# Decoder layer: k and v of cross-attention computed inside self-attention, and a cross-attention loop with the context product two pairs behind the scores

## The reference, cut to what matters

```
# self-attention: 16 heads of 32
scores = (q k^T + q . pos_emb[l-r] + k . pos_emb[l-r]) / sqrt(32)
ctx    = softmax(scores) v ;  h = ctx @ Wo + bo + x ; layer norms -> x1
# cross-attention: 16 heads of 64, batch 8 x 512 seen as (8, 512)
q = x1 Wq[h] + bq[h] ; k = context Wk[h] + bk[h] ; v = context Wv[h] + bv[h]
out = softmax(causal(q k^T / sqrt(64))) v ;  out @ Wo + bo ; add, norm
```

## Time and profile before

| | |
|---|---|
| median of 3 runs | 4272.65 us (4272.12 to 4275.99) |
| the profiled execution | 4274.03 us, span 4272.1 us, granted clock 0.942 |
| PE busy | 3681.4 us (86%) |
| DVE, ACT, POOL busy | 2230.7 (52%), 1678.6 (39%), 1859.8 us (44%) |
| self-attention, 0 to 1700 us | PE busy 1435 us, DMA share 0.96 |
| cross-attention, 1905 to 3107 us | PE busy 1154 us, DMA share 0.53 |

### The profile page before, as it was taken

The page is one execution under the profiler, slowest core; times in us unless marked ns, Lnnn a source line. Parts: engine busy times, 40 slices in busy tenths (PEclk is TensorE's granted clock), DMA queues, the critical chain, the costliest instruction groups (busy, mean ns, idle before and its releaser), DMA issues. The chain is left out here.

```text
span 4272.1 us, 67667 instructions
## 1 busy us (share of the span) xinstructions
PE 3681.4 (86%) x19584; PEld 2298.4 (54%) x19584; DVE 2230.7 (52%) x6128; ACT 1678.6 (39%) x3639; POOL 1859.8 (44%) x1684
## 2 busy tenths in 40 slices
PE   6988888888888886769999999999989987788686
PEld 4766666667676674325556666655545552122244
DVE  4666676767666665773554555455523231111155
ACT  4666666666666664333333333333312110000023
POOL 3766666667676665433444444444511100000012
PEclk9999999999999998989999999999989998898798
DMA  6999999999999997455555555555355328999723
GB/s 246 399 375 391 386 385 374 386 369 386 373 388 377 385 387 295 142 176 194 180 180 175 173 172 176 179 178 180 128 183 186 107 74 350 420 421 421 290 79 118
DMA packets 544321, 1151.74 MB, mean 270 GB/s; under 512 B 34240, under 2 KB 206912, under 8 KB 494912
## 3 DMA queue, kind: packets, MB, share of 16 engines
q1 hardware_dynamic: 539520, 1141.13, 71.7%
q10 hardware_dynamic: 4032, 7.34, 0.5%
q0 software_dynamic: 512, 0.26, 0.0%
HBM read 745.46 MB, written 403.18 MB: 269 GB/s over the span
## 5 line engine op out<-in xcount | busy, mean ns | idle before, releaser
L433 POOL TENSOR_SCALAR a_sc<-a_sc,a_inv 128x512 f32<-128x512 f32 x512 | 818.5, 1602 | 383.1 <-DVE a_inv L383 313.1
L1004 POOL TENSOR_SCALAR b_sc<-b_sc,b_inv 128x128 f32<-128x128 f32 (+3 forms) x512 | 549.6, 1082 | 657.5 <-DVE b_inv L957 657.5
L284 ACT ACTIVATE a_stage_q<-a_ps_q 128x640 f32<-128x640 f32 x512 | 360.0, 703 | 469.8 <-PE a_ps_q L201 442.5
L962 DVE COPY b_pt<-b_ps_t 128x128 f32<-128x128 f32 (+3 forms) x512 | 250.2, 489 | 547.3 <-PE b_ps_t L863 547.3
L390 DVE COPY a_pt<-a_ps_t 128x512 f32<-128x512 f32 x512 | 353.6, 691 | 280.3 <-PE a_ps_t L187 242.3
L376 DVE CUSTOM_DVE_ANT_0 a_sc<-a_ps_s,a_rq 128x512 f32<-128x512 f32 x512 | 353.9, 691 | 197.2 <-PE a_ps_s L177 145.0
L918 ACT ACTIVATE b_sc<-b_sc,b_mx 128x128 f32<-128x128 f32 (+3 forms) x512 | 281.0, 550 | 446.7 <-DVE b_mx L951 446.7
L274 ACT ACTIVATE a_sc<-a_sc,a_mx 128x512 f32<-128x512 f32 x512 | 370.5, 724 | 77.5 <-DVE a_mx L376 75.9
L175 PE MATMUL a_ps_s<-a_ks,a_qs 128*128 128x512 f32 x512 | 261.2, 510 | 139.4 <-DMA a_rk<-band_k 103.9
L284 ACT ACTIVATE a_stage_k<-a_ps_k 128x640 f32<-128x640 f32 x512 | 359.1, 701 | 30.4 <-DMA band_k<-a_stage_k 30.4
L187 PEld LDWEIGHTS a_ps_t<-a_ident,a_sc 128*128 128x128 f32 x2048 | 249.9, 145 | 218.2 <-issue 201.2
(11 more groups left out here) (200 smaller groups left out, 6159.5 us busy)
## 6 DMA issues: line engine op xcount, KB each, us to landing
band_q<-a_stage_q SPq DMA_DIRECT2D x128, 1280.0 KB, 9.0
band_k<-a_stage_k SPq DMA_DIRECT2D x128, 1280.0 KB, 11.6
a_rk<-band_k SPq DMA_DIRECT2D x128, 1024.0 KB, 13.9
a_rq<-band_q SPq DMA_DIRECT2D x256, 512.0 KB, 14.6
d_w<-in_e_W SPq DMA_DIRECT2D x32, 4096.0 KB, 36.9
b_xT<-x1T SPq DMA_DIRECT2D x64, 1024.0 KB, 5.7
b_cT<-in_ctxT SPq DMA_DIRECT2D x64, 1024.0 KB, 8.4
d_wg<-in_e_Wg SPq DMA_DIRECT2D x16, 4096.0 KB, 28.0
```

Of the source, the lines that this page charges most:

```text
L284: act.activation(st[h % 2][:, t, :].rearrange("p (a n) -> p a n", a=2), src[:, :, 0:WIN // 2], ACT.Copy).then_inc(sem[f"a_{kind}_staged"], 1)
L433: pool.tensor_scalar(sc[n][:, :], sc[n][:, :], inv[:, n:n + 1], None, ALU.mult)\
L1004: pool.tensor_scalar(sc[i][:, 0:width(i)], sc[i][:, 0:width(i)], inv[:, i:i + 1], None, ALU.mult).then_inc(sem["b_normed"], 1)
```

## The change

Four things are changed together.

1. The k and v of cross-attention are projected in self-attention. Each quad takes two pairs: 16 parts m (four for k of the first pair, four for its v, and the same for the second), put at the ticks in `KV_AT`. Each result is copied by ScalarE to one tile kv, which SyncE stores to DRAM scratch. ScalarE issues the loads of the weights (okv, 512 KB each) and, once in four quads, of the context (oc, 1 MB).
2. To find PSUM for it, ps_q and ps_k share three banks, and the bands are four products of 384, 256, 256 and 384 columns. To find SBUF, pt holds two heads instead of four, so that the context product of self-attention is made in two halves (ticks 11 and 3), each with the sums of r = 0, 1 and r = 2, 3 in rows of their own, which VectorE then adds.
3. cross_attention projects only q. k and v are loaded from the scratch, the bias of v is added by ScalarE when it copies the context product out.
4. The loop of cross_attention is staggered otherwise: in pair n TensorE does the scores of n, the transposes of n-1, the context product of n-2 at i = 0, and the projection of q for n+1 at i = 1, 2, 5 and 7. sc, mx, sm and inv are doubled, pt is single.

```diff
-Q_AT, K_AT, HI_AT = [5, 6, 7, 8], [10, 11, 12, 13], [9, 14]
+Q_AT, K_AT, HI_AT = {5: [0], 6: [1], 7: [2], 8: [3]}, {13: [0, 1], 14: [2, 3]}, [9, 15]
+CX_AT, CX_OUT_AT = [HALF + LAG_A, LAG_A], [HALF + LAG_A + 1, LAG_A + 1]
+KV_AT = [[1, 2, 3, 4, 5, 6, 7, 8, 9, 10, 11, 11, 12, 13, 14, 15], list(range(NT)), list(range(NT)),
+         [0, 1, 2, 3, 4, 4, 5, 6, 7, 7, 8, 9, 10, 10, 11, 12]]
...
+            def store_kv(g, n):
+                sp.wait_ge(sem["a_kv_out"], 4 * g + n + 1)
+                settle()
+                sp.dma_start(dr[("b_k", "b_v")[n % 2]](2 * g + n // 2), kv[:, :]).then_inc(sem["a_kv_stored"], 16)
             def quad(g, j):
                 for h in range(HQ):
+                    if inside(g):
+                        store_kv(g, h)
                     if inside(g + 1):
                         write(g + 1, (j + 1) % 4, h)
...
+            def project_kv(g, j, m):
+                c, kind, n = m // 8, m // 4 % 2, m % 4
+                if m == 0 and j == 0:
+                    pe.wait_ge(sem["a_oc_in"], 4 * g + 16)
+                if m % 8 == 0:
+                    pe.wait_ge(sem[f"a_okv_in{c}"], 16 * g + 16)
+                if n == 0 and counts(4 * g + m // 4):
+                    pe.wait_ge(sem["a_kv_out"], 4 * g + m // 4)
+                if kind == 0:
+                    mm = pe.matmul(ps_o[:, :], okv[c][:, 0, n, :], oc[:, n, :], start=(n == 0), stop=(n == K4 - 1))
+                else:
+                    for k in range(K4):
+                        mm = pe.matmul(ps_o[:, n * P:(n + 1) * P], oc[:, k, n * P:(n + 1) * P], okv[c][:, 1, k, :],
+                                       start=(k == 0), stop=(k == K4 - 1))
...
+            def kv_out(g, j, n):
+                act.wait_ge(sem["a_kv_ready"], 4 * g + n + 1)
+                if counts(4 * g + n):
+                    act.wait_ge(sem["a_kv_stored"], 16 * (4 * g + n))
...
+                if n == 3 and j == 3 and inside(g + 1):
+                    act.dma_start(oc[:, :, :], dr["a_oc"](g + 1)).then_inc(sem["a_oc_in"], 16)
+                if n % 2 and inside(g + 1):
+                    act.dma_start(okv[n // 2][:, :, :, :].rearrange("p a k n -> p (a k n)"),
+                                  dr["b_wkv"](2 * ((j + 1) % 4) + n // 2)).then_inc(sem[f"a_okv_in{n // 2}"], 16)
...
 cross_attention, SyncE
+            def load(n, j):
+                if not early(n, 2):
+                    sp.wait_ge(sem["b_q_ready"], n - 1)
+                    settle()
+                    sp.wait_ge(sem["b_score"], NP * (n - 1))
+                    settle()
+                s = sem[f"b_in{j % 2}"]
+                sp.dma_start(wq[j % 2][:, :, :].rearrange("p k n -> p (k n)"), dr["b_wq"](n)).then_inc(s, 16)
+                sp.dma_start(xT[j % 2][:, :, :], dr["x1T"](n)).then_inc(s, 16)
+                if not early(n, 4):
+                    sp.wait_ge(sem["b_cx_out"], n - 3)
+                    settle()
+                sp.dma_start(cols[j][:, :], dr["b_cols"](n)).then_inc(s, 16)
+                sp.dma_start(kT[j % 2][:, :], dr["b_k"](n)).then_inc(s, 16)
+            def load_v(n, j):
+                if not early(n, 2):
+                    sp.wait_ge(sem["b_cx_ready"], n - 1)
+                    settle()
+                sp.dma_start(v[j % 2][:, :, :].rearrange("p t n -> p (t n)"), dr["b_v"](n))\
+                    .then_inc(sem[f"b_v_in{j % 2}"], 16)
+            def store(n, j):
+                sp.wait_ge(sem["b_cx_out"], n + 1)
...
+            def pair(n, j):
+                if inside(n + 1) and not early(n, 1):
+                    load(n + 1, (j + 1) % 4)
+                if not early(n, 2):
+                    store(n - 2, (j - 2) % 4)
+                if inside(n + 1) and not early(n, 1):
+                    load_v(n + 1, (j + 1) % 4)
...
 cross_attention, TensorE
+            def project_q(n, j, k):
+                if k == 0:
+                    pe.wait_ge(sem[f"b_in{j % 2}"], (n - j % 2) * 32 + 64)
+                    if not early(n, 1):
+                        pe.wait_ge(sem["b_q_out"], n)
...
+            def pair(n, j):
+                for i in range(NP):
+                    if i in (0, 4) and inside(n):
+                        scores(n, j, i)
+                    if i == 0 and not early(n, 2):
+                        context(n - 2, j % 2)
+                    if not early(n, 1):
+                        turn(n - 1, (j - 1) % 4, i)
+                    if i in Q_OF_PAIR and inside(n + 1):
+                        project_q(n + 1, (j + 1) % 4, Q_OF_PAIR.index(i))
...
 cross_attention, ScalarE and VectorE
+            def pair(n, j):
+                for i in range(NP):
+                    if inside(n):
+                        softexp(n, j, i)
+                    if i == 3 and not early(n, 2):
+                        cx_out(n - 2, (j - 2) % 4)
+                if inside(n + 1):
+                    q_out(n + 1, (j + 1) % 4)
...
+            def pair(n, j):
+                for half in (0, 4):
+                    if inside(n):
+                        for i in range(half, half + 4):
+                            add_max(n, j, i)
+                    for i in range(half, half + 4):
+                        if not early(n, 1):
+                            pt_out(n - 1, i)
+                        if inside(n) and i % 2:
+                            invert(n, j, i - 1)
+                            invert(n, j, i)
...
+Q_OF_PAIR = [1, 2, 5, 7]
```

More of the change, by code:

```diff
@@ L757, in cross_attention, with steps, inside, early @@
         ident = sb("b_ident", [P, P])
-        ps_p = ps("b_ps_p", [P, 2, 512])
         ps_s = [ps(f"b_ps_s{i}", [P, 512]) for i in range(4)]
         ps_t = [ps(f"b_ps_t{i}", [P, 512]) for i in range(2)]
+        ps_q = ps("b_ps_q", [P, 512])
+        ps_c = ps("b_ps_c", [P, 512])
         def width(i):
             return (i // 2 + 1) * P
+        def steps(e, pair):
+            for n in range(4):
+                pair(n, n)
+            with e.Fori(4, PAIRS - 4, 4) as n:
+                for j in range(4):
+                    pair(n + j, j)
+            for n in range(PAIRS - 4, PAIRS + 1):
+                pair(n, n % 4)
+        def inside(n):
+            return not isinstance(n, int) or 0 <= n < PAIRS
+        def early(n, k):
+            return isinstance(n, int) and n < k
         block = ctx.enter_context(nc.Block())
@@ L799, in _ @@
+            load(0, 0)
             sp.dma_start(ident[:, :], dr["ident"]).then_inc(sem["b_const_in"], 16)
             sp.dma_start(mask[:, :], dr["mask"]).then_inc(sem["b_const_in"], 16)
[L801 to L810, removed]
@@ L892, in _ @@
-            pe.wait_ge(sem["b_const_in"], 32)
-            for u in range(6):
-                unit(0, 0, u)
-            pe_pair(0, 0, first=True)
-            with pe.Fori(1, PAIRS - 1, 2) as n:
-                pe_pair(n, 1)
-                pe_pair(n + 1, 0)
-            pe_pair(PAIRS - 1, 1, last=True)
-            for i in range(NP - LAG, NP):
-                turn(PAIRS - 1, i)
-            context(PAIRS - 1, 1)
+                    if i in (0, 4) and inside(n):
+                        scores(n, j, i)
@@ new lines, in pair @@
+                    if i == 0 and not early(n, 2):
[4 more added lines that the diff above has]
+                        project_q(n + 1, (j + 1) % 4, Q_OF_PAIR.index(i))
+            for k in range(K4):
+                project_q(0, 0, k)
+            pe.wait_ge(sem["b_const_in"], 32)
+            steps(pe, pair)
+            context(PAIRS - 1, (PAIRS - 1) % 4)
@@ L937, in _, with add_max @@
+            act.wait_ge(sem["b_in0"], 64)
+            q_out(0, 0)
+            steps(act, pair)
+            cx_out(PAIRS - 1, (PAIRS - 1) % 4)
         @block.vector
         def _(dve):
[L939 to L945 removed]
+            def add_max(n, j, i):
```

383 lines of the change are left out of this document (173 added, 210 removed).

## The result

The changed kernel takes 4961.61 us (median of 4 runs, 4955.81 to 4975.27) against 4272.39 us before: a ratio of 1.1617, 95% interval 1.1589 to 1.1645, 16% slower. The forecast was 4830 us, range 4580 to 5000, slower with a chance of 0.93. The profiled execution is the slowest of the four, 4975.27 us around a span of 4973.3. Both stages that the change touches became longer: project_norm's first load, which marks the end of self-attention, was issued at 1698.3 us before and at 2061.8 after (+363), and the 63 periods of the pairs took 1131.8 us before and 1482.5 after (+351).

A forecast was written before the change was run, and what follows sets the result against it. Self-attention was taken as short of DMA time (0.99 in the steady part), cross-attention as short of TensorE time (1154 of 1202 us). 4274 + 275 for self-attention + 280 for cross-attention = 4829, said as 4830 us; range 4580 to 5000.

The forecast's parts named there:

- The wait for the load: Cross-attention: TensorE's project_q waits in every pair for the next pair's load, issued late in SyncE's queue; 7.4 us idle.
- the landing: Cross-attention: time from the load's first issue until all four of its DMAs have landed, taken as 7.1 us.
- q_out: Cross-attention: the next pair's scores wait for ScalarE's copy of q, whose last chunk ends the pair; 0.95 us a pair.
- the turns: Cross-attention: TensorE waits at turn(6) for VectorE's four add_max and a pt copy; 1.05 us a pair.
- The clock: Cross-attention: TensorE's clock falls after the load wait in every pair; 2.2 us a pair of full-speed work lost.
- The 10.80: Cross-attention: TensorE's time left in a pair once k, v and the wait for the v copy are removed, in us.
- The quad: Self-attention: period of one quad, 50.4 us before, forecast 58.6 us with the k and v of two pairs added.
- bound of 62.3: Self-attention: upper bound of the quad in us, with present clock loss kept and a full 1 us per kv_out.
- The kv copies: Self-attention: each kv_out on ScalarE waits for the store before it, chiefly at j = 3; within 0.6 us a quad.
- The second pt wait: Self-attention: the halved context product waits for a pt copy twice, adding 1.4 us a quad to the existing 1.45.
- The DMA floor of 56.1 us: Self-attention: least quad time the DMA engines allow, 50.4 x 0.99 plus 6.2 us for the added loads and stores.
- The rival that the load is not on the path: Cross-attention: load issued early enough, load and clock waits vanish; 12.8 us a pair, total 4224 us, faster; chance 0.06.

The follow-up runs named there:

- warm: Changed kernel, with TensorE doing eight unread products per cross-attention pair, from the fourth on, before its wait for the load: 4864.12 us.
- load_ahead: Changed kernel, with the load of pair n+2 put ahead of the v load of n+1 in SyncE's queue, last four loop pairs unrolled: 4281.64 us.
- kv_spread: Changed kernel, with the fourth quad's kv copies 4, 4 and 3 ticks apart instead of 3, 3 and 3, next context load two ticks later: 4909.59 us.

## Why the prediction was right, by its own steps

**The wait for the load** decided, as said. It was found by writing down what SyncE's queue waits for, in order, and in which pair TensorE does each of these things. 569.8 us of waits in 63 pairs, and -680 us when the order is changed, show it. Its size was 7.4 us and came to 9.05. The term that was too small is the landing: from the first issue at 3015.09 there were 2.53 us to the issue of k, and from there to its landing 6.8 us in the median of all 64 (7.2 in the pair shown), so 9.3 instead of 7.1. The release took less than the 0.54 allowed: 0.17 us from the end of the context product to the first issue. The 7.1 had been scaled from a load whose xT came second; here k is fifth, and 0.6 us had been taken off for the longer rows of wq. The trace does not bear that out: wq lands after 2.8 us in the median, and landed after 2.9 before.

**q_out and the turns**: 54.9 / 63 = 0.87 us against 0.95, 39.0 / 63 = 0.62 against 1.05. The turns, sized 0.43 too high, gave back a part of the 1.65 that the load was too low, which is luck. **The clock**: 23.53 - 10.80 - 9.05 - 0.87 - 0.62 = 2.2 us against 2.2. This is what is left over and not a measurement; warm shows about 1.3 of it. The 10.80 are borne out by load_ahead, where 10.80 + (54.7 + 38.9 + 21.2) / 63 = 12.6 us stand against 12.54. All that lies outside the two periods came to -13 us against nothing: 363 + 351 - 13 = 701, the difference of the two spans.

**The quad** was to be 58.6 us; it is 61.7 over the stage, and 63.1 in the loop, which is over the prediction's own bound of 62.3. The stage grew by 363 us against 275: the direction was right, the size a quarter too small. (The bound is not what its words add up to: 58.0, 2.6 us of clock and 1 us for each of four kv copies are 64.6.) In the iteration from 809 to 1061.5, TensorE's busy time of 231.0 is 4 x 55.1 = 220.4 and 10.6 more. The granted clock of 0.97 accounts for some (1 - 0.97) x 252.5 = 8 us of these (an estimate), so the 14.0 us a quad that are moved were right to within a microsecond. Above it lie 8.4 us of standstill at the loop's end, 9.0 us behind kv copies (6.6 for a_kv, 2.4 for a_stage_q behind it) and 2.9 us for pt.
- The standstill was not in the sum. Its 35.2 us were in the trace of before, in the same view as the earlier trace rows, and the prediction does not mention them. They were covered by the DMA engines, and the change took most of this cover away: five of them cost 64 us here and 11 there.
- The kv copies were named, with the right quad (j = 3), but sized within 0.6 us a quad; they took 2.2 and some clock. kv_spread got 52 us of them back.
- The second pt wait was sized at 1.4 us on top of 1.45; both together are 21.8 / 32 = 0.7 us a quad, in 31 waits and not two a quad.
- The DMA floor of 56.1 us did not matter; share 0.91, not 0.95. TensorE is busy 0.91 of the iteration, where above 0.93 was forecast.

The rival that the load is not on the path was priced at 12.8 us a pair and 4224 us in all. load_ahead made it real: 12.54 us and 4281.64, the difference being the quad's (+363 against the 275 in its sum).

## What to carry to other kernels

When a loop is staggered anew, write for each queue that runs in order what its steps wait for, and in which turn of the loop those things happen: a load that stands behind another load's release is as late as that release, however early its own conditions hold. When work moves from a stage bound by one resource into one bound by another, look for waits that the old bound was covering; they are in the old trace with their full length and cost little or nothing there.

## What the runs showed of the hardware that was not expected

At the end of each iteration of self-attention's loop the engines stood still together, TensorE for 5.8 to 6.8 us once in 252 us in the changed kernel and for 5.7 to 6.2 us before, and none of it showed in the unrolled stretches or in the shorter loop of cross-attention. In the pair shown the clock was back at its higher level 4.8 us after work had resumed from a wait of 9.3 us, in a stage where TensorE was busy only 56% of the time. Eight products (7.0 us) in the gap held it at 1.00 in 36 of 63 windows of a pair's length, not in all. And a 256 KB load landed 6.8 us after its issue with a 1 MB load ahead of it in the queue, 3.4 us without.
